# Attention in a decoder layer: projections cut into pieces, one rope step moved back, and the output weights' low parts taken from VectorE to GpSimd

## The chip, the cores and the metric

One core of a Trainium2 chip runs the whole kernel. The metric is device time in microseconds (us) of one execution; three runs of the kernel before gave 1610.72, 1613.61 and 1617.08, median 1613.61. A difference of 0.5% is about 8 us.

## What is computed

The reference is one pre-norm decoder layer on x of shape (4, 512, 512) in float32: causal grouped-query attention, a cross attention to 64 memory tokens, and a mixture of 8 experts. The change touches the first part alone:

```python
def _L0_attn_ref(x, Wq, Wk, Wv, Wo):                  # 32 query heads, 8 key/value heads, 64 wide
    q = (x @ Wq.T).reshape(B, L, HQ, HD)
    k = (x @ Wk.T).reshape(B, L, HKV, HD)
    v = (x @ Wv.T).reshape(B, L, HKV, HD)
    q = _rope(q)
    k = _rope(k)
    ...
    attn = jnp.einsum('bkgqd,bkld->bkgql', qh, kh) * SCALE
    attn = jnp.where(causal[None, None, None], attn, -jnp.inf)
    p = jax.nn.softmax(attn, axis=-1)
    out = jnp.einsum('bkgql,bkld->bkgqd', p, vh)
    ...
    return out @ Wo.T

x = x + _L0_attn_ref(_layernorm(x, axis=-1), L0_attn_Wq, L0_attn_Wk, L0_attn_Wv, L0_attn_Wo)
```

## The kernel before

The attention is written out by hand, engine by engine, with semaphores between them. Its outer loop is over the 8 key/value heads ("groups", g), then over the 4 batches (b), then over the 4 query heads (h) of that group: 8 x 16 = 128 **steps** c, each on one head of 64 columns and 512 rows. Every engine's program walks the same steps in `pe_group`, `act_group`, `dve_group` and `pool_group`; in step c the score matmuls are those of head c + 1, the transposes of P those of head c - 1 (in the code `d = c - 1`, with its batch `db` and its head `dh`), and P times v that of head c - 2. What stands in one engine's program is done in that order, and no engine overtakes.

Float32 accuracy is had by splitting a value into a high part (rounded by a copy on ScalarE, ACT) and a low part (value minus high part, one subtraction on VectorE, DVE, or GpSimd, POOL), and multiplying in two or three passes on TensorE (PE). The work of one step:

- PE: transposes of unit 2 of P (2 blocks, `pe_ptrans` L218), scores (`pe_scores`, 8 matmuls, L208), a projection (`pe_proj`, 12 matmuls, L185) where one falls in the step, transposes of units 0 and 1 (8 blocks, L218), P times v (`pe_pv`, 8 matmuls, L235), and one of the four 128-row tiles of a batch's output projection (`pe_wo`, 6 matmuls, L247).
- DVE: four masked row blocks (`dve_masked` L422), the low parts of P transposed (`dve_pt`, `pt_lo`, L410), the reciprocal of row sums (L429), sums for the output (`dve_oadd` L475, `dve_woacc` L485), low parts of q (L447, L448), of o and v, and the first half of rope (`dve_rope_in` L440, L441: times cosine, and a shuffle into `rot`).
- ACT: the high parts (`act_split` L306) and the exponentials (`act_exp` L313).
- POOL: the second half of rope (`pool_rope` L537, L539: `rot` times sine, then the sum), the softmax scaling of P (`pool_norm` L546), the low part of k (`pool_k_lo` L553).

A group has three projections for each batch, each made one batch ahead: r = 2 (k and v together) in step h = 0, r = 0 and r = 1 (two query heads each) in steps h = 1 and h = 2. Each of the three has a rope step behind it, numbered by h; the third is the one of step h = 2. Step h = 3 has no projection; there v is transposed (`pe_vt` L195). All projections go through one PSUM bank, `PJ_BANK`, so a projection waits until rope has read the one before. Rope's second halves wait on one `rot` buffer.

Weights of a group come in by DMA while the group before runs: `w1` (for q, k, v) and `w2` (the group's 256 rows of the output weights, 512 columns). There is one buffer for `w2`: `act_w2` can write its high parts only after the last output tile of the group before (step h = 1 of b = 1, c = 5), and PE needs high and low parts for the first output tile of the group, in step h = 2 of b = 1 (c = 6). In the kernel before the low parts are `dve_w2`, in that step on DVE:

```python
                if h == 2 and next_batch:
                    dve_q_lo(dve, m + 1, 1, (b + 1) % 2)
                if dh == 1 and db == 1:
                    dve_w2(dve, g)
                if h < 3 and next_batch:
                    dve_rope_in(dve, m + 1, h, (b + 1) % 2)
```

PE waits for them in front of that tile, with `pe.wait_ge(s["w2_lo_done"], 2 * g + 2)`. Groups 1 to 6 are a loop of two turns (`Fori`), three groups in each turn.

Of the kernel before, what the change touches and what calls it, by code (L numbers as in the profile page):

```python
# [15 lines left out]
F32 = mybir.dt.float32  # L16
# [9 lines left out]
P = 128  # L26
# [38 lines left out]
W1_SLOTS = {(2, 1): 2, (2, 2): 0, (2, 3): 1}  # L65

# [33 lines left out]
def decoder_layer(nc, x, ctx, ctx_cols, mem_mask, wqkv, wo_rows, router_cols, router_b, gu_w, gu_b, down_w, down_b,  # L100
                  cos_t, sin_t, causal_t, ident_t, iota_t, out):
    stack = ExitStack()
    with stack:
# [76 lines left out]
        def pe_proj(pe, b, r):  # L180

            first = True
            for c in range(DC):
                for sp, mp in PASSES:
                    last = nc.tensor.matmul(PJ_BANK[:, :], w1[sp][:, c, r * P:(r + 1) * P], xn[mp][:, c, b * L:(b + 1) * L],  # L185
                                            start=first, stop=(c == DC - 1 and (sp, mp) == PASSES[-1]))
                    first = False
            last.then_inc(s["proj_done"], 1)

        def pe_vt(pe, m):  # L190

            pe.wait_ge(s["vt_done"], m + 1)
            settled(pe)
            for j in range(QB):
                last = nc.tensor.transpose(PJ_BANK[:, j * HD:(j + 1) * HD], v_t[:, j * P:(j + 1) * P], ident[HD:P, HD:P])  # L195
            last.then_inc(s["v_tr"], 1)
# [55 lines left out]
        def pe_group(pe, g, r):  # L252
# [4 lines left out]
            for c in range(HEADS + (isinstance(g, int) and g == GROUPS - 1)):  # L257
# [12 lines left out]
                d_before_last = not (isinstance(g, int) and g == 0 and db < 2)  # L270
                if d_begun:
# [3 lines left out]
                if h < 3 and b == 3 and next_batch:  # L275
                    pe.wait_ge(s["w1_lo_done"], 3 * g + 4 + h)
                if h == 0 and next_batch:
                    pe.wait_ge(s["v_lo_done"], m + 1)
                    pe_proj(pe, (b + 1) % B, 2)
                if h == 1 and next_batch:  # L280
                    pe.wait_ge(s["rope_in"], 3 * m + 4)
                    pe.wait_ge(s["vt_done"], m + 2)
                    pe_proj(pe, (b + 1) % B, 0)
                if h == 2 and next_batch:
                    pe.wait_ge(s["rope_in"], 3 * m + 5)
                    pe_proj(pe, (b + 1) % B, 1)
                if h == 3 and next_batch:
# [9 lines left out]
                if dh in (1, 2) and d_last:  # L297
                    if dh == 1 and db == 1:
                        pe.wait_ge(s["w2_lo_done"], 2 * g + 2)
                    pe_wo(pe, dm - 1, (db - 1) % 2, dh - 1)  # L300
                if dh == 0 and d_before_last:
                    pe_wo(pe, dm - 2, db % 2, 3)
# [65 lines left out]
        def act_group(act, g, r):  # L368

            for c in range(HEADS + (isinstance(g, int) and g == GROUPS - 1)):  # L370
# [41 lines left out]
        def dve_masked(dve, n, hb):  # L412
# [3 lines left out]
            for i in (3, 2, 1, 0):  # L416
# [1279 lines left out]
```

## Time and profile before

| | |
|---|---|
| median of three runs | 1613.61 us |
| the profiled execution, its own time | 1613.59 us |
| its span in the trace | 1611.8 us |
| busy share of PE, DVE, ACT, POOL in the span | 92%, 85%, 66%, 54% |
| mean granted TensorE clock | 0.958 of 2.4 GHz |

Times in the trace count from the start of the span. The attention takes the span up to about 1045 us, the rest is the cross attention and the experts. A group of 16 steps takes 123 us. Timeline rows give the start, the time that one instruction took (for several merged ones the stretch from the first start to the last end), engine, line, output and inputs, shape, count, and in brackets how long the engine had been idle and who released it. Matmuls are pipelined, so the length of a run of them is read from its first start to the next run's first start.

### The profile page before, as it was taken

The page shows a single profiled execution, that of the slowest core. Times are in us where ns is not written, and L with a number is a line of the kernel's source. Part 1 is how long each engine was busy: PE and PEld are TensorE (multiplying, and loading weights), DVE is VectorE, ACT ScalarE, POOL GpSimd, SP SyncE. Part 2 cuts the span into 40 slices and gives each one's busy share as a digit, 9 for nine tenths or more (in the row PEclk, how much of TensorE's full clock was granted, in tenths as well). Part 3 has the DMA queues.
Part 4 walks back from the last instruction along what each step waited for, and adds up shares of the span by engine and source line. Part 5 has one row for each costly group of instructions (what it writes and reads, how often), then busy time and mean ns, then how long its engine had stood idle before and what let it go on. Part 6 is the DMA issues. An engine that isn't in the chain of part 4 may idle for free. (4 is left out here: it accounts for less than half of the span.)

```text
span 1611.8 us, 31199 instructions
## 1 busy us (share of the span) xinstructions
PE 1484.4 (92%) x8952; PEld 1308.7 (81%) x8952; DVE 1374.7 (85%) x3583; ACT 1056.9 (66%) x2464; POOL 870.1 (54%) x1024
## 2 busy tenths in 40 slices
PE   5789999999999899999999999769879999999998
PEld 4678888888888778887887887658769999999997
DVE  7788898898988798898898888668868888988896
ACT  3677777777777677777777777533136666666664
POOL 6657657557657556656656666157413343334432
PEclk9899999999999999999999999975579999999999
DMA  4000000000000000000000000042448888777761
GB/s 178 1 14 21 1 14 21 1 14 21 1 14 21 3 14 16 6 14 2 21 4 12 1 1 1 1 139 99 133 124 226 227 230 227 228 210 211 202 184 46
DMA packets 61950, 117.10 MB, mean 73 GB/s; under 512 B 22718, under 2 KB 22846, under 8 KB 61776
## 3 DMA queue, kind: packets, MB, share of 16 engines
q1 hardware_dynamic: 51328, 98.05, 19.1%
q0 software_dynamic: 10304, 16.94, 5.2%
q8 instruction: 77, 1.26, 0.3%
q14 instruction: 97, 0.79, 0.1%
q10 hardware_dynamic: 144, 0.07, 0.0%
HBM read 101.89 MB, written 20.51 MB: 76 GB/s over the span
## 5 line engine op out<-in xcount | busy, mean ns | idle before, releaser
L313 ACT ACTIVATE probs<-probs,neg_max 128x512 f32<-128x512 f32 (+3 forms) x512 | 281.6, 551 | 46.5 <-DVE neg_max L422 44.2
L546 POOL TENSOR_SCALAR probs<-probs,row_inv 128x512 f32<-128x512 f32 (+3 forms) x512 | 264.2, 534 | 44.5 <-DVE row_inv L429 44.5
L537 POOL TENSOR_TENSOR rot<-rot,sin 128x512 f32<-128x512 f32 (+1 forms) x96 | 123.7, 1289 | 303.8 <-DVE rot L441 299.4
L218 PE MATMUL bank<-ident,probs 128*128 128x128 f32 x1280 | 185.1, 275 | 59.9 <-DVE pt_lo L410 50.4
L410 DVE TENSOR_TENSOR pt_lo<-bank,pt_hi 128x512 fp32r<-128x512 f32 (+1 forms) x384 | 216.2, 590 | 26.9 <-ACT pt_hi L306 26.9
L1265 POOL DMA_INDIRECT out<-ctx_raw,idx x46 | 93.1, 2024 | 268.6 <-ACT ctx_raw L1420 217.3
L306 ACT ACTIVATE pt_hi<-bank 128x512 fp32r<-128x512 f32 (+1 forms) x384 | 186.0, 518 | 72.8 <-PE bank L218 64.5
L422 DVE CUSTOM_DVE_ANT_0 probs<-bank,causal 128x512 f32<-128x512 f32 (+3 forms) x512 | 219.8, 482 | 10.3 <-issue 3.3
L218 PEld LDWEIGHTS bank<-ident,probs 128*128 128x128 f32 x1280 | 150.5, 141 | 95.2 <-DVE pt_lo L410 55.3
L1347 PE MATMUL bank<-xt_hi,gu_hi 128*128 128x256 f32 x736 | 208.8, 284 | 3.5 <-issue 1.9
L1347 PE MATMUL bank<-xt_hi,gu_lo 128*128 128x256 f32 x736 | 206.9, 281 | 0.0
L1347 PE MATMUL bank<-xt_lo,gu_hi 128*128 128x256 f32 x736 | 206.9, 281 | 0.0
L208 PE MATMUL bank<-k_hi,q_st 128*128 128x256 f32 (+2 forms) x512 | 172.7, 348 | 2.9 <-DVE xn_lo L410 2.9
L235 PE MATMUL bank<-pt_hi,v_st 128*128 128x256 f32 (+2 forms) x512 | 171.1, 345 | 1.6 <-DVE pt_lo L410 1.6
L208 PE MATMUL bank<-k_lo,q_st 128*128 128x256 f32 (+2 forms) x512 | 157.2, 328 | 0.0
L235 PE MATMUL bank<-pt_lo,v_st 128*128 128x256 f32 (+2 forms) x512 | 155.4, 326 | 0.0
L185 PE MATMUL bank<-xn_hi,w_hi 128*128 128x512 f32 x384 | 152.6, 397 | 0.3 <-ACT v_and_o L306 0.3
L185 PE MATMUL bank<-xn_lo,w_hi 128*128 128x512 f32 x384 | 151.4, 394 | 0.0
L185 PE MATMUL bank<-xn_hi,w_lo 128*128 128x512 f32 x384 | 151.0, 393 | 0.0
L1347 PEld LDWEIGHTS bank<-xt_hi,gu_hi 128*128 128x128 f32 x736 | 139.8, 190 | 7.4 <-issue 4.2
L1347 PEld LDWEIGHTS bank<-xt_lo,gu_hi 128*128 128x128 f32 x736 | 140.0, 190 | 3.0
L1347 PEld LDWEIGHTS bank<-xt_hi,gu_lo 128*128 128x128 f32 x736 | 139.7, 190 | 0.0
(204 smaller groups left out, 3920.7 us busy)
## 6 DMA issues: line engine op xcount, KB each, us to landing
gu_raw<-in_gate_up SPq DMA_DIRECT2D x92, 512.0 KB, 3.8
dn_raw<-in_down SPq DMA_DIRECT2D x92, 256.0 KB, 3.8
w_raw<-in_wqkv SPq DMA_DIRECT2D x8, 768.0 KB, 4.1
w_raw<-in_wo_rows SPq DMA_DIRECT2D x8, 512.0 KB, 3.5
h_rows<-ln_h SPq DMA_DIRECT2D x16, 256.0 KB, 2.0
out<-x_res SPq DMA_DIRECT2D x4, 1024.0 KB, 5.0
x_res<-in_x SPq DMA_DIRECT2D x3, 1024.0 KB, 11.1
ctx_raw<-in_ctx SPq DMA_DIRECT2D x2, 512.0 KB, 6.3
```

The lines of the kernel that those rows point to most:

```text
L185: last = nc.tensor.matmul(PJ_BANK[:, :], w1[sp][:, c, r * P:(r + 1) * P], xn[mp][:, c, b * L:(b + 1) * L], start=first, stop=(c == DC - 1 ...
L208: last = nc.tensor.matmul(S_BANK[k][:, at:at + cols], q_st[:, h, i * P:(i + 1) * P], kk[:, kb, 0:cols], start=(a == 0), stop=(a == 1))
L218: last = nc.tensor.transpose(T_BANK[u % 2][:, k * P:(k + 1) * P], probs[:, hb, P_AT[i] + j * P:P_AT[i] + (j + 1) * P], ident[:, :])
L235: last = nc.tensor.matmul(dst, v_st[:, vb, j, :], rhs, start=(j == 0 and a == 0), stop=(j == QB - 1 and a == 1))
L306: nc.scalar.activation(dst, src, ACT.Copy).then_inc(sem_, 1)
L313: nc.scalar.activation(row, row, ACT.Exp, bias=neg_max[:, hb, i:i + 1], scale=-1.0, accum_out=row_sum[:, hb, i:i + 1]).then_inc(s["exp_don ...
L410: nc.vector.tensor_tensor(dst, src, hi.bitcast(F32), ALU.subtract).then_inc(sem_, 1)
L422: nc.vector.tensor_tensor_reduce(out=probs[:, hb, P_AT[i]:P_AT[i] + (i + 1) * P], in0=S_BANK[k][:, at:at + (i + 1) * P], in1=causal[:, (QB ...
L537: nc.gpsimd.tensor_tensor(rot[0:rows, :], rot[0:rows, :], sin[0:rows, :], ALU.mult).then_inc(s["rot_sin"], 1)
L546: nc.gpsimd.tensor_scalar(row, row, row_inv[:, hb, i:i + 1], 0.0, ALU.mult, ALU.add).then_inc(s["pnorm_done"], 1)
L1265: nc.gpsimd.indirect_dma_start(out=out_rows, out_offset=bass.IndirectOffsetOnAxis(ap=idx[:, 2 * tau + h:2 * tau + h + 1], axis=0), in_=y[: ...
L1347: last = nc.tensor.matmul(GU_BANK[u % 3][:, side * TILE:(side + 1) * TILE], gu[sp_][:, ib, c, side, :], xts[mp][:, k, c, :], start=first, ...
```

## The change

1. **Projections in pieces.** `pe_proj` takes a range of its 12 matmuls. The k and v projection is begun in step h = 3 of the batch before (9 matmuls) and ended in h = 0 (3); r = 0 is begun at the end of h = 0 (6) and ended in h = 1 (6); r = 1 is begun at the end of h = 1 (3) and ended in h = 2 (9). Each of the steps then has 9 projection matmuls.
2. **Output tiles.** Tiles 1 and 3 move ahead of the transposes of their steps, as tile 2 was; tile 0 alone (step h = 2) stays behind P times v.
3. **v.** Its transposes go through a bank of the P transposes, `T_BANK[1]`, and move ahead of the scores of step h = 3; its high and low parts move with them, and the next transposes into that bank wait for them.
4. **Rope.** In step h = 2 alone DVE's half (the third rope step) moves behind the low parts of P. The copy of its result on ACT and the low part of q on DVE move from the next h = 0 into h = 3.
5. **DVE order.** The low part of P's unit 2 moves between the second and the third masked block. `act_o` moves to the start of the next step.
6. **w2.** Its low parts move from DVE to POOL (`pool_w2`), behind `pool_norm` of step c = 6. POOL's low parts of w1 get a wait for the low part of q in two of three slots.
7. **No loop.** Groups 1 to 6 are written out.

```diff
+KV_FIRST, Q01_FIRST, Q23_FIRST = 9, 6, 3
...
-        def pe_vt(pe, m):
+        def pe_vt(pe, m, heads_before):
             pe.wait_ge(s["vt_done"], m + 1)
             settled(pe)
+            wait(pe, s["pt_lo_done"], heads_before and 3 * heads_before - 1)
...
+            if u == 1 and n % G == 2 and n < HEADS * GROUPS - G:
+                pe.wait_ge(s["v_lo_done"], n // G + 2)
...
+                if h == 3 and next_batch:
+                    pe_vt(pe, m + 1, dn_)
                 if more:
                     pe_scores(pe, n + 1, m if h < G - 1 else m + 1, (h + 1) % G, (b + (h == G - 1)) % 2)
...
                 if h == 0 and next_batch:
-                    pe.wait_ge(s["v_lo_done"], m + 1)
-                    pe_proj(pe, (b + 1) % B, 2)
+                    pe_proj(pe, (b + 1) % B, 2, KV_FIRST)
                 if h == 1 and next_batch:
...
-                    pe_proj(pe, (b + 1) % B, 0)
+                    pe_proj(pe, (b + 1) % B, 0, Q01_FIRST)
                 if h == 2 and next_batch:
...
+                    pe_proj(pe, (b + 1) % B, 1, Q23_FIRST)
+                if h == 3 and batch_after:
+                    if b == 2:
+                        pe.wait_ge(s["w1_lo_done"], 3 * g + 4)
                     pe.wait_ge(s["rope_in"], 3 * m + 6)
-                    pe_vt(pe, m + 1)
+                    pe_proj(pe, (b + 2) % B, 2, 0, KV_FIRST)
                 if dh == 3 and d_last:
                     pe_wo(pe, dm - 1, (db - 1) % 2, 2)
+                if dh == 2 and d_last:
+                    pe_wo(pe, dm - 1, (db - 1) % 2, 1)
+                if dh == 0 and d_before_last:
+                    pe_wo(pe, dm - 2, db % 2, 3)
                 if d_here:
                     pe_ptrans(pe, dn_, (r + d) % 3, 0)
                     pe_ptrans(pe, dn_, (r + d) % 3, 1)
...
+                if dh == 1 and d_last:
+                    if db == 1:
                         pe.wait_ge(s["w2_lo_done"], 2 * g + 2)
+                    pe_wo(pe, dm - 1, (db - 1) % 2, 0)
+                if h == 0 and next_batch:
+                    if b == 3:
+                        pe.wait_ge(s["w1_lo_done"], 3 * g + 5)
+                    pe.wait_ge(s["rope_in"], 3 * m + 4)
+                    pe.wait_ge(s["vt_done"], m + 2)
+                    pe_proj(pe, (b + 1) % B, 0, 0, Q01_FIRST)
+                if h == 1 and next_batch:
...
+                    pe.wait_ge(s["rope_in"], 3 * m + 5)
+                    pe_proj(pe, (b + 1) % B, 1, 0, Q23_FIRST)
...
-                if h == 0 and begun and front:
-                    act_rope(act, m, 2, b % 2)
-                if h in (1, 2) and next_batch:
+                e = d - 1
+                eb, eh = divmod(e, G)
+                if eh % 2 == 0 and not (isinstance(g, int) and g == 0 and e < 1):
+                    act_o(act, HEADS * g + e - 1, B * g + eb if eh else B * g + eb - 1, (e // 2 - 1) % 4)
+                if h == 3 and next_batch:
+                    act_v(act, m + 1, (b + 1) % 2)
+                if h and next_batch:
                     act_rope(act, m + 1, h - 1, (b + 1) % 2)
...
+        def pool_w2(pool, g):
             for k in range(2):
-                dve.wait_ge(s["w2_hi_done"], 2 * g + k + 1)
-                dve_lo(w2[1][:, k, :], w2_raw[:, k, :], w2[0][:, k, :], s["w2_lo_done"])
+                pool.wait_ge(s["w2_hi_done"], 2 * g + k + 1)
+                nc.gpsimd.tensor_tensor(w2[1][:, k, :], w2_raw[:, k, :], w2[0][:, k, :].bitcast(F32), ALU.subtract).then_inc(s["w2_lo_done"], 1)
...
                 if more:
-                    dve_masked(dve, n + 1, (r + c + 1) % 3)
+                    dve_masked(dve, n + 1, (r + c + 1) % 3, (3, 2))
                 if d_begun:
                     dve_pt(dve, dn_ - 1, (d + 1) % 2, 2)
+                if more:
+                    dve_masked(dve, n + 1, (r + c + 1) % 3, (1, 0))
...
-                if dh == 1 and db == 1:
-                    dve_w2(dve, g)
-                if h < 3 and next_batch:
+                if h == 3 and next_batch:
+                    dve_v(dve, m + 1, (b + 1) % 2)
+                if h >= 2 and next_batch:
+                    dve_q_lo(dve, m + 1, h - 1, (b + 1) % 2)
+                if h < 3 and next_batch and h != 2:
                     dve_rope_in(dve, m + 1, h, (b + 1) % 2)
...
                     dve_pt(dve, dn_, d % 2, 0)
                     dve_pt(dve, dn_, d % 2, 1)
+                if h == 2 and next_batch:
+                    dve_rope_in(dve, m + 1, h, (b + 1) % 2)
...
                 if more:
                     pool_norm(pool, n + 1, (r + c + 1) % 3)
+                if dh == 1 and db == 1:
+                    pool_w2(pool, g)
                 if (b, h) in W1_SLOTS and not (isinstance(g, int) and g == GROUPS - 1):
+                    if h < 3:
+                        pool.wait_ge(s["q_lo_done"], 2 * m + 2 + h)
                     w1_lo(nc.gpsimd, pool, g + 1, W1_SLOTS[b, h])
...
-                with pe.Fori(0, (GROUPS - 2) // 3) as q:
-                    for i in range(1, 4):
-                        pe_group(pe, 3 * q + i, i % 3)
+                for g in range(1, GROUPS - 1):
+                    pe_group(pe, g, g % 3)
```

What the diff does to the order, at three places. The square brackets name the semaphores that an instruction waits for.

POOL, step c = 6 of a group (shown for group 0), before: the second half of the third rope step (`rot`, `rope`), then the softmax scaling of one head (`probs`).

```order
L537 TENSOR_TENSOR rot<-rot,sin 128x512 [waits rope_in]
L539 TENSOR_TENSOR rope<-rope,rot 128x512 [waits rot_sin]
L546 TENSOR_SCALAR probs<-probs,row_inv 128x512 [waits recip_done]
L546 TENSOR_SCALAR probs<-probs,row_inv 128x384
L546 TENSOR_SCALAR probs<-probs,row_inv 128x256
L546 TENSOR_SCALAR probs<-probs,row_inv 128x128
```

The same step after:

```order
L556 TENSOR_TENSOR rot<-rot,sin 128x512 [waits rope_in]
L558 TENSOR_TENSOR rope<-rope,rot 128x512 [waits rot_sin]
L565 TENSOR_SCALAR probs<-probs,row_inv 128x512 [waits recip_done]
L565 TENSOR_SCALAR probs<-probs,row_inv 128x384
L565 TENSOR_SCALAR probs<-probs,row_inv 128x256
L565 TENSOR_SCALAR probs<-probs,row_inv 128x128
L480 TENSOR_TENSOR w_lo<-w_raw,w_hi 128x512 [waits w2_hi_done] x2
```

The two low parts of w2 are new on POOL and stand last in the step, behind the rope sum and the scaling.

DVE, step h = 2 of b = 0 in group 0, from the low part of P's unit 2 on, before (at c = 6 the two `w_lo` of w2 stand between `q_st` and `rope`):

```order
L410 TENSOR_TENSOR pt_lo<-bank,pt_hi 128x256 [waits pt_hi_done]
L410 TENSOR_TENSOR o_lo<-o_f,o_hi 128x512 [waits o_hi_done]
L447 TENSOR_TENSOR q_st<-rope,q_st 64x512 [waits rope_hi]
L448 TENSOR_TENSOR q_st<-rope,q_st 64x512
L440 TENSOR_TENSOR rope<-bank,cos 128x512 [waits k_lo_done,rope_sum,proj_done]
L441 STREAM_SHUFFLE rot<-bank 128x512
L429 RECIPROCAL row_inv<-row_sum 128x4 [waits exp_done]
L410 TENSOR_TENSOR pt_lo<-bank,pt_hi 128x512 [waits pt_hi_done] x2
```

and the end of that step after:

```order
L427 TENSOR_TENSOR o_lo<-o_f,o_hi 128x512 [waits o_hi_done]
L464 TENSOR_TENSOR q_st<-rope,q_st 64x512 [waits rope_hi]
L465 TENSOR_TENSOR q_st<-rope,q_st 64x512
L446 RECIPROCAL row_inv<-row_sum 128x4 [waits exp_done]
L427 TENSOR_TENSOR pt_lo<-bank,pt_hi 128x512 [waits pt_hi_done] x2
L457 TENSOR_TENSOR rope<-bank,cos 128x512 [waits k_lo_done,rope_sum,proj_done]
L458 STREAM_SHUFFLE rot<-bank 128x512
```

The shuffle into `rot`, for which POOL's first row above waits, went from ahead of the reciprocal to behind the two low parts of P.

ACT, step h = 3, after (before, the two `q_st` copies stood in the next step, h = 0, and `v_st` behind `pt_hi` of units 0 and 1):

```order
L323 ACTIVATE pt_hi<-bank 128x256 [waits ptrans_done]
L323 ACTIVATE v_st<-bank 128x4x64 [waits pv_done,v_tr]
L323 ACTIVATE q_st<-rope 64x512 [waits scores_done,rope_sum]
L323 ACTIVATE q_st<-rope 64x512
L330 ACTIVATE probs,row_sum<-probs,neg_max 128x512 [waits masked_done]
L330 ACTIVATE probs,row_sum<-probs,neg_max 128x384 [waits masked_done]
L330 ACTIVATE probs,row_sum<-probs,neg_max 128x256 [waits masked_done]
L330 ACTIVATE probs,row_sum<-probs,neg_max 128x128 [waits masked_done]
L323 ACTIVATE pt_hi<-bank 128x512 [waits pv_done,ptrans_done]
```

The copies of the third rope result (`q_st`, released by POOL's `rope_sum`) now stand ahead of the step's exponentials and of `pt_hi`.

## Rows read from the trace of the kernel before

**Rows 1.** Busy time by engine in a stretch of the attention: PE, PEld, DVE, ACT, POOL, clock.

```profile
160.00:540.00 380.00, 361.11 (x2077) 312.49 (x2075) 339.10 (x894) 289.17 (x733) 241.14 (x307) 1.00 0.04 12
```

**Rows 2.** Waits of PE from 60 to 1046 us: total us, times, longest.

```profile
PE bank L218 <- DVE pt_lo L410: 50.4, 48, 3.7
```

**Rows 3.** Timeline of PE: v's transposes of three batches, and a step h = 2.

```profile
288.71 0.46 PE L195 MATMUL bank<-ident,v_and_o 64*128 64x64 f32 x4
...
309.52 0.38 PE L218 MATMUL bank<-ident,probs 128*128 128x128 f32 x2
...
311.03 0.40 PE L185 MATMUL bank<-xn_hi,w_hi 128*128 128x512 f32 x1
...
313.77 1.03 PE L218 MATMUL bank<-ident,probs 128*128 128x128 f32 x8
...
315.94 0.40 PE L247 MATMUL bank<-w_hi,o_hi 128*128 128x512 f32 x1
...
317.32 0.38 PE L218 MATMUL bank<-ident,probs 128*128 128x128 f32 x2
...
318.93 0.46 PE L195 MATMUL bank<-ident,v_and_o 64*128 64x64 f32 x4
...
320.55 1.09 PE L218 MATMUL bank<-ident,probs 128*128 128x128 f32 x8 [1.16 <-DVE pt_lo L410]
...
534.84 0.46 PE L195 MATMUL bank<-ident,v_and_o 64*128 64x64 f32 x4
```

**Rows 4.** Timeline of PE around the loop's turn, after group 3.

```profile
552.19 0.49 PE L218 MATMUL bank<-ident,probs 128*128 128x128 f32 x2 [2.61 <-DVE pt_lo L410]
...
554.88 0.63 PE L185 MATMUL bank<-xn_hi,w_hi 128*128 128x512 f32 x1
...
558.11 1.03 PE L218 MATMUL bank<-ident,probs 128*128 128x128 f32 x8
...
571.04 0.46 PE L195 MATMUL bank<-ident,v_and_o 64*128 64x64 f32 x4
```

**Rows 5.** Waits of all engines, 60 to 1060 us: the one on ACT without a releaser.

```profile
ACT pt_hi L306 <- issue: 5.5, 1, 5.5
```

**Rows 6.** Busy time by engine behind that turn; the column after POOL is the granted clock.

```profile
552.50:555.50 3.00, 3.00 (x12) 2.71 (x11) 2.77 (x8) 2.40 (x7) 2.92 (x6) 0.50 0.00 0
```

**Rows 7.** Timeline of PE and ACT at c = 6 of a group, begun at 339.74.

```profile
339.74 0.38 PE L218 MATMUL bank<-ident,probs 128*128 128x128 f32 x2
...
340.43 1.14 ACT L306 ACTIVATE w_hi<-w_raw 128x512 fp32r<-128x512 f32 x2
...
341.88 1.27 ACT L306 ACTIVATE q_st<-rope 64x512 fp32r<-64x512 f32 x2
343.18 0.73 ACT L313 ACTIVATE probs<-probs,neg_max 128x512 f32<-128x512 f32 x1
...
345.38 1.05 ACT L306 ACTIVATE pt_hi<-bank 128x512 fp32r<-128x512 f32 x2
```

**Rows 8.** Timeline of DVE in the same step.

```profile
340.73 0.69 DVE L422 CUSTOM_DVE_ANT_0 probs<-bank,causal 128x512 f32<-128x512 f32 x1
...
342.71 0.80 DVE L410 TENSOR_TENSOR o_lo<-o_f,o_hi 128x512 fp32r<-128x512 f32 x1
...
344.97 1.29 DVE L410 TENSOR_TENSOR w_lo<-w_raw,w_hi 128x512 fp32r<-128x512 f32 x2
346.18 0.68 DVE L440 TENSOR_TENSOR rope<-bank,cos 128x512 f32<-128x512 f32 x1
...
347.50 1.26 DVE L410 TENSOR_TENSOR pt_lo<-bank,pt_hi 128x512 fp32r<-128x512 f32 x2
```

**Rows 9.** Timeline of POOL in the same step.

```profile
347.61 1.28 POOL L537 TENSOR_TENSOR rot<-rot,sin 128x512 f32<-128x512 f32 x1 [4.62 <-DVE rot L441]
...
350.24 2.06 POOL L546 TENSOR_SCALAR probs<-probs,row_inv 128x512 f32<-128x512 f32 x4
```

**Rows 10.** Low parts of weights by tile, 180 to 540 us: ns min/median/max.

```profile
L457 POOL TENSOR_TENSOR w_lo<-w_raw,w_hi x9: 1283/1297/1724, 251.3 to 511.3; 128x512 fp32r<-128x512 f32 x9
```

More of the change, by code:

```diff
@@ L178, in pe_ln, with pe_proj @@
             last.then_inc(s["lnt_done"], 1)
[L180 to L188, printed above, removed]
-        def pe_vt(pe, m):
+        def pe_proj(pe, b, r, begin=0, end=3 * DC):
+            for n in range(begin, end):
+                c, (sp, mp) = n // 3, PASSES[n % 3]
+                last = nc.tensor.matmul(PJ_BANK[:, :], w1[sp][:, c, r * P:(r + 1) * P], xn[mp][:, c, b * L:(b + 1) * L],
+                                        start=(n == 0), stop=(n == 3 * DC - 1))
+            if end == 3 * DC:
+                last.then_inc(s["proj_done"], 1)
+        def pe_vt(pe, m, heads_before):
             pe.wait_ge(s["vt_done"], m + 1)
             settled(pe)
+            wait(pe, s["pt_lo_done"], heads_before and 3 * heads_before - 1)
             for j in range(QB):
-                last = nc.tensor.transpose(PJ_BANK[:, j * HD:(j + 1) * HD], v_t[:, j * P:(j + 1) * P], ident[HD:P, HD:P])
+                last = nc.tensor.transpose(T_BANK[1][:, j * HD:(j + 1) * HD], v_t[:, j * P:(j + 1) * P], ident[HD:P, HD:P])
             last.then_inc(s["v_tr"], 1)
@@ L410, in dve_lo, with dve_masked @@
             nc.vector.tensor_tensor(dst, src, hi.bitcast(F32), ALU.subtract).then_inc(sem_, 1)
-        def dve_masked(dve, n, hb):
+        def dve_masked(dve, n, hb, blocks=(3, 2, 1, 0)):
             wait(dve, s["ptrans_done"], 3 * n - 6)
-            for i in (3, 2, 1, 0):
+            for i in blocks:
                 k = (2, 2, 1, 0)[i]
@@ L521, in dve_group @@
                     dve_pt(dve, dn_, d % 2, 1)
+                if h == 2 and next_batch:
+                    dve_rope_in(dve, m + 1, h, (b + 1) % 2)
                 if dh == 3 and d_last:
                     dve_woacc(dve, dm - 1, (db - 1) % B, 2)
-                if h == 3 and next_batch:
-                    dve_v(dve, m + 1, (b + 1) % 2)
+                if dh == 2 and d_last:
+                    dve_woacc(dve, dm - 1, (db - 1) % B, 1)
+                if dh == 0 and d_before_last:
+                    dve_woacc(dve, dm - 2, (db - 2) % B, 3)
                 if d_begun:
                     dve_oadd(dve, dn_ - 1, (d - 1) % 2, HEADS // 2 * g + (d - 1) // 2)
-                if dh in (1, 2) and d_last:
-                    dve_woacc(dve, dm - 1, (db - 1) % B, dh - 1)
-                if dh == 0 and d_before_last:
-                    dve_woacc(dve, dm - 2, (db - 2) % B, 3)
+                if dh == 1 and d_last:
+                    dve_woacc(dve, dm - 1, (db - 1) % B, 0)
         def pool_rope(pool, m, r, mb):
@@ L607, in _ @@
                 sp_w2(sp, 0)
-                with sp.Fori(1, GROUPS) as g:
+                for g in range(1, GROUPS):
                     sp_w1(sp, g)
@@ L667, in _ @@
                 act_group(act, 0, 0)
-                with act.Fori(0, (GROUPS - 2) // 3) as q:
-                    for i in range(1, 4):
-                        act_group(act, 3 * q + i, i % 3)
+                for g in range(1, GROUPS - 1):
+                    act_group(act, g, g % 3)
                 act_group(act, GROUPS - 1, (GROUPS - 1) % 3)
@@ L709, in _ @@
                 dve_group(dve, 0, 0)
-                with dve.Fori(0, (GROUPS - 2) // 3) as q:
-                    for i in range(1, 4):
-                        dve_group(dve, 3 * q + i, i % 3)
+                for g in range(1, GROUPS - 1):
+                    dve_group(dve, g, g % 3)
                 dve_group(dve, GROUPS - 1, (GROUPS - 1) % 3)
@@ L738, in _ @@
                 pool_group(pool, 0, 0)
-                with pool.Fori(0, (GROUPS - 2) // 3) as q:
-                    for i in range(1, 4):
-                        pool_group(pool, 3 * q + i, i % 3)
+                for g in range(1, GROUPS - 1):
+                    pool_group(pool, g, g % 3)
                 pool_group(pool, GROUPS - 1, (GROUPS - 1) % 3)
```

31 lines of the change are left out of this document (7 added, 24 removed).

## Prediction

> **What bounds the kernel now.** I read the busy shares by stretch first. In the steady attention PE is busy 361 of 380 us (95%), DVE 339 (89%), ACT 289, POOL 241 [rows 1]: PE is the bound, DVE close behind, POOL has room. The granted clock is full there. Next the waits of PE: 48 waits for a low part of P, 50.4 us in all, are nearly everything [rows 2]. So the question is what PE's own work takes and what stands between.
>
> The timeline of PE answers it. A step h = 2 runs without a hole from 309.52 to 317.32, 7.80 us: unit 2 and scores 1.51, twelve projection matmuls 2.74, the transposes of units 0 and 1 with P times v 2.17, an output tile 1.38 [rows 3]. Step h = 3 has no projection but v's transposes (0.46): 7.80 - 2.74 + 0.46 = 5.52. A batch without any wait is then 3 x 7.80 + 5.52 = 28.92 us, a group 115.68. What it takes is read from v's transposes: 288.71 to 318.93 is 30.22 for a batch without weight work, of which 1.16 is the one wait in front of the transposes in h = 3, where PE has too little to do while DVE still masks; 288.71 to 534.84 is two groups, 123.07 each [rows 3]. **The loss is 7.39 us a group**, 59 in eight. That is all that a better order can give back.
>
> One thing comes on top: the loop's turn. The batch from 534.84 to 571.04 takes 36.20 instead of 30.22 [rows 3, 4], 5.98 more. ACT stands 5.5 us without any releaser there [rows 5], PE 2.61 [rows 4], and behind it the clock is at 0.50, 1.2 GHz [rows 6], so that unit 2 and scores take 2.69 instead of 1.51 and the projection 3.23 instead of 2.74 [rows 3, 4]: 1.7 us is the price of a slow clock after a gap.
>
> **The change, part by part.** I write times from the start of a step on PE.
>
> *Pieces, output tiles, v.* No matmul is added or taken away. Four steps of 9 projection matmuls (2.05 us) replace three of 12; every step is about 7.12, h = 3 with v's transposes 7.58. The batch's sum stays 28.92. What can change is the waits.
>
> *Loop written out:* -6.0 us, once. The two groups from 288.71 to 534.84 [rows 3] run through code written out inside a turn, at one pace, so I cost the longer code at nothing.
>
> *The third rope step.* It now starts on DVE behind the low parts of P. In a plain batch's h = 2 POOL's queue ahead (rope, scaling, low part of k, rope: 2.63 + 2.06 + 2.6 + 2.63 [rows 9, 10] from the first rope's shuffle, some 5.8 into h = 0) lets ACT copy q at about 1.8; the copies take 1.30 and the exponentials 2.20 [rows 7], so pt_hi begins at 5.3, its low parts are done at 7.1 (0.6 for one pt_hi, 1.2 for two low parts [rows 8]) and rope's half on DVE, 1.24 [rows 8], at 8.3. POOL's half ends at 8.4 + 2.63 = 11.1. In h = 3 ACT must now copy that result before its exponentials: copies to 12.5, exponentials to 14.7, one pt_hi 15.2, its low part 15.9, and for that PE waits at the next h = 0, which it would reach at 7.12 + 7.58 = 14.7. **A wait of about 1.3 us returns, at another place**, where 1.16 stood before. Bounds: nothing if ACT's part comes 1.3 earlier, 2.6 if it comes as much later. I take 1.3: every term of it is a row.
>
> *w2 on POOL.* DVE loses 2 x 0.6 us at c = 6 (344.97 to 346.18 [rows 8]); POOL gets two subtractions at 1.30 [rows 10]. POOL has the room on average. But look at what stands ahead of them in its queue, and what waits. POOL reaches w2 in step c = 6 behind the third rope's half and the scaling; that rope waits for DVE's shuffle, which now comes behind the low parts of P; and PE needs w2's low parts in the same step, behind P times v:
> - ACT: the w2 copies begin at 0.1 (o_hi, ahead of them before, moves behind them). Before, from them to pt_hi of unit 0 it took 340.43 to 345.38, 4.95 [rows 7]; with o_hi in it (0.53, half of the two pt_hi copies of that shape [rows 7]) pt_hi begins at 5.6.
> - DVE: masks from 1.0 (340.73 - 339.74 [rows 7, 8]), to o_lo 1.98, o_lo and the low part of q 2.26, free at 5.2; low parts of P from 6.2 (one pt_hi is 0.53) to 7.4; rope 1.24, to 8.6 [rows 8].
> - POOL: rope 2.63 (347.61 to 350.24), to 11.3 with 0.09 in front; scaling 2.06, to 13.4 [rows 9]; w2 2.6 [rows 10], to 16.0.
> - PE is ready at 1.51 + 2.05 + 2.17 = 5.7 and **stands 10.3 us**, once a group.
>
> Bounds: if ACT held nobody up, pt_lo would follow q's low part at 5.2 and all ends 1.0 earlier, 9.3; if ACT came a set of exponentials later (2.2), 12.5. In either case DVE's order alone puts the shuffle behind PE's transposes. In that gap ACT, DVE and POOL work off what they owe, so the 1.3 us of this batch vanishes. After it PE starts at the slow clock: I take the 1.7 us of the loop's turn; the ends are 0 and 3.4.
>
> *w1.* After, its copies stand at ends of steps where ACT next waits for rope anyway, and POOL's new wait for q's low part (5.2 of h = 2) ends before its next rope can begin (8.4): nothing. If that cover were gone, 1.3 us, one subtraction [rows 10], once a group.
>
> *Sum.* A group loses 10.3 + 1.7 + 3 x 1.3 = 15.9 us instead of 7.4, 8.5 more; eight are 68; the loop gives back 6. 1613.6 + 62 = **1676 us**. The profiled execution took 1613.59 us, 1.8 more than its span, and the median is 1613.61, so nothing has to be converted. The rest of the kernel is left alone.
>
> **What the Trainium skill says.** The GPSIMD Engine Reference, sections 3.1 and 4.1, gives VectorE for elementwise work on a tile, GpSimd being 1.96 times slower in a two-input add: a rule against this move. By it the pair would take 1.96 x 1.29 = 2.5 us (an estimate from that page) where the rows of POOL give 2.6, and the sum would be 1 us less; trace and page agree that the move doubles this work, but its length is a quarter of the gap and its place in the queue the rest. On the clock, TensorE: Matmul & The Clock Gate, Part 1, says that "the default state is throttled, and activity releases the throttle"; the row at 0.50 behind a 2.61 us gap agrees. By that rule each of the eight gaps must pay, as I have it; without it the sum would be 14 us less.
>
> **Rivals.**
> 1. *The late rope costs nothing in plain batches.* For it: steps are balanced, DVE's mask order brings P's unit 2 forward. Against: ACT's exponentials in h = 3 now wait for POOL. 24 waits of 1.3 less: 1676 - 31 = 1645.
> 2. *The waits are larger than I count.* DVE is at 89%, and a late step pushes the next. Plain waits of 2.6 instead of 1.3: 1676 + 31 = 1707.
> 3. *Faster: w2 is in time.* If POOL had w2 done by 5.7 us of c = 6, all the loss could go: 1613.6 - 59 - 6 = 1549. For it: POOL was idle 4.62 us in just that step [rows 9]. Against: it was idle in front of the rope, waiting for the shuffle, and w2 stands behind that. The point that decides: with no other wait left, gap and slow clock together would have to be under 7.4 + 0.75 = 8.1 us; my lowest gap alone is 9.3.
> 4. *PE does not wait there after all*, because w2's low parts come from the group before. The code writes them anew for each group and PE's wait counts them, so I give this little; it falls together with the third.
>
> **How the numbers follow.** Forecast 0.74, first rival 0.12, second 0.10, third and fourth 0.04. The range 1640 to 1710 takes in the first two rivals and, for the forecast, gaps of 9.3 to 12.5 (-8 to +18) and clock prices of 0 to 3.4 (-14 to +14), not all at one end. Slower by over 0.5% (8 us, what a measurement of this kernel can tell from no change) 0.95; within 0.5% 0.02, a gap near the deciding point; faster 0.03.
>
> **What would show it.** PE's waits: eight of about 10 us in front of the first output tile, for `w_lo`, released by POOL's L480; POOL's `w_lo` starting some 13.4 us after the step does; 1.2 GHz behind each; the waits for `pt_lo` moved from the transposes of units 0 and 1 to unit 2 of h = 0, about 1.3 us, 24 of them; no 5.5 us hole on ACT. It is wrong if `w_lo` on POOL starts before the rope's half, if the gaps are under 8 us, or if a batch without weights takes 29 us or over 32.

## The result, and the profile after

The changed kernel takes 1688.74 us (median of 4 runs, 1686.61 to 1690.56), the kernel before beside it 1615.34 (4 runs). The ratio is 1.0444 with an interval of 1.0415 to 1.0473: **4.4% slower, 73 us**, where +62 had been forecast. The profiled execution took 1687.77 us, 1.9 more than its span of 1685.9; the span grew by 74.1.

The page after: the line of the span, the busy shares, and of the costliest groups the output projection on PE (after the second bar: idle time in front of the group, and what ended most of it).

```profile
span 1685.9 us, 28647 instructions
...
PE 1505.6 (89%) x8952; PEld 1321.4 (78%) x8952; DVE 1368.5 (81%) x3567; ACT 1066.6 (63%) x2464; POOL 914.0 (54%) x1040
...
L252 PE MATMUL bank<-w_hi,o_hi 128*128 128x512 f32 x256 | 105.8, 413 | 83.3 <-POOL w_lo L480 80.2
```

POOL's share is 54%, as it was before. An average did not see the loss; the last line does. PE stood 80.2 us in front of output tiles, and the end of POOL's low parts of w2 released it.

Waits of all engines after, 60 to 1125 us (total us, times, longest):

```profile
PE bank L252 <- POOL w_lo L480: 80.2, 8, 10.7
ACT q_st L323 <- POOL rope L558: 67.2, 25, 3.1
...
PE bank L223 <- DVE pt_lo L427: 30.2, 26, 2.7
```

Eight waits of 10.0 us are new, one a group. The 48 waits for a low part of P, 50.4 us [rows 2], are now 26, 30.2 us; 21 of them, three between each two of the eight, are 1.0 to 1.1 us long, and the other five lie at the two ends of the attention. ACT's 5.5 us without a releaser [rows 5] is gone from this list. The second line is nearly new on ACT: its copies of q wait for POOL's rope, which before they did once, for 1.6 us.

Now step c = 6 of group 2, which starts on PE at 360.66; it answers to [rows 7, 8, 9]. PE, from v's transposes of the batch before on:

```profile
337.66 0.46 PE L198 MATMUL bank<-ident,v_and_o 64*128 64x64 f32 x4
...
360.66 0.38 PE L223 MATMUL bank<-ident,probs 128*128 128x128 f32 x2
...
366.28 0.28 PE L240 MATMUL bank<-pt_lo,v_st 128*128 128x256 f32 x1
376.48 0.79 PE L252 MATMUL bank<-w_hi,o_hi 128*128 128x512 f32 x1 [9.92 <-POOL w_lo L480]
...
379.21 0.63 PE L223 MATMUL bank<-ident,probs 128*128 128x128 f32 x2
379.77 0.69 PE L198 MATMUL bank<-ident,v_and_o 64*128 64x64 f32 x4
...
382.21 0.40 PE L187 MATMUL bank<-xn_hi,w_hi 128*128 128x512 f32 x1
...
409.58 0.46 PE L198 MATMUL bank<-ident,v_and_o 64*128 64x64 f32 x4
...
470.59 0.46 PE L198 MATMUL bank<-ident,v_and_o 64*128 64x64 f32 x4
```

DVE and then POOL in the same step:

```profile
366.73 1.29 DVE L427 TENSOR_TENSOR pt_lo<-bank,pt_hi 128x512 fp32r<-128x512 f32 x2 [0.30 <-ACT pt_hi L323]
367.94 0.68 DVE L457 TENSOR_TENSOR rope<-bank,cos 128x512 f32<-128x512 f32 x1
...
368.54 0.72 DVE L458 STREAM_SHUFFLE rot<-bank 128x512 f32<-128x512 f32 x1
```

```profile
369.34 1.26 POOL L556 TENSOR_TENSOR rot<-rot,sin 128x512 f32<-128x512 f32 x1 [4.53 <-DVE rot L458]
370.69 1.26 POOL L558 TENSOR_TENSOR rope<-rope,rot 128x512 f32<-128x512 f32 x1
371.92 2.06 POOL L565 TENSOR_SCALAR probs<-probs,row_inv 128x512 f32<-128x512 f32 x4
373.94 2.48 POOL L480 TENSOR_TENSOR w_lo<-w_raw,w_hi 128x512 fp32r<-128x512 f32 x2
```

Read them as one chain. POOL stands idle 4.53 us until the shuffle ends, then does rope, scaling and w2 in its queue's order; PE, done at 366.56 (366.28 + 0.28), starts its tile when w2 ends. The change moved the chain's start, the shuffle, back, and put at the chain's end the low parts for which PE waits; before, PE's list has one wait for them in the whole kernel, of 1.1 us, ended by DVE.

Busy time by engine in four stretches of this step (PE, PEld, which is PE's weight load, DVE, ACT, POOL, granted clock, DMA share, GB/s):

```profile
366.40:371.00 4.60, 0.16 (x2) 0.00 (x0) 3.12 (x7) 1.37 (x3) 1.58 (x2) 1.00 0.00 0
371.20:376.40 5.20, 0.00 (x0) 0.00 (x0) 0.00 (x0) 0.00 (x0) 5.20 (x7) 0.50 0.00 0
376.50:381.30 4.80, 4.80 (x14) 3.57 (x15) 0.69 (x1) 1.19 (x3) 0.00 (x0) 0.50 0.36 113
381.40:386.00 4.60, 4.60 (x26) 3.95 (x25) 3.95 (x13) 2.92 (x9) 0.12 (x1) 1.00 0.00 0
```

For 5.2 us POOL alone of the five works. The clock is at 0.50 (1.2 GHz) for that time and for 4.8 us more, in which PE is busy throughout.

### The profile page after: what moved, and what is told of

It is laid out like the page before. It is cut to its first block and busy times, and to the rows that moved or that the text cites. A ratio compares the mean times of both kernels' runs of the same rounds, so it can differ in the third digit from the quotient of the medians.

```text
span 1685.9 us, 28647 instructions
## 1 busy us (share of the span) xinstructions
PE 1505.6 (89%) x8952; PEld 1321.4 (78%) x8952; DVE 1368.5 (81%) x3567; ACT 1066.6 (63%) x2464; POOL 914.0 (54%) x1040
## 5 line engine op out<-in xcount | busy, mean ns | idle before, releaser
L565 POOL TENSOR_SCALAR probs<-probs,row_inv 128x512 f32<-128x512 f32 (+3 forms) x512 | 288.9, 585 | 119.3 <-DVE row_inv L446 119.3
L439 DVE CUSTOM_DVE_ANT_0 probs<-bank,causal 128x512 f32<-128x512 f32 (+3 forms) x512 | 228.3, 482 | 20.5 <-PE bank L211 18.6
L223 PE MATMUL bank<-ident,probs 128*128 128x128 f32 x1280 | 185.2, 275 | 30.5 <-DVE pt_lo L427 30.2
L252 PE MATMUL bank<-w_hi,o_hi 128*128 128x512 f32 x256 | 105.8, 413 | 83.3 <-POOL w_lo L480 80.2
L187 PE MATMUL bank<-xn_hi,w_hi 128*128 128x512 f32 x384 | 156.3, 407 | 3.0 <-ACT v_and_o L323 2.4
L502 DVE TENSOR_TENSOR x_res<-bank,x_res 128x512 f32<-128x512 f32 x128 | 87.0, 680 | 80.2 <-PE bank L252 80.2
```

Of the source, the lines that this page charges most:

```text
L223: last = nc.tensor.transpose(T_BANK[u % 2][:, k * P:(k + 1) * P], probs[:, hb, P_AT[i] + j * P:P_AT[i] + (j + 1) * P], ident[:, :])
L439: nc.vector.tensor_tensor_reduce(out=probs[:, hb, P_AT[i]:P_AT[i] + (i + 1) * P], in0=S_BANK[k][:, at:at + (i + 1) * P], in1=causal[:, (QB ...
L565: nc.gpsimd.tensor_scalar(row, row, row_inv[:, hb, i:i + 1], 0.0, ALU.mult, ALU.add).then_inc(s["pnorm_done"], 1)
```

## The experiments

The ratios are to the kernel before, run beside each; its medians there were 1614.5 to 1616.6 us, so times of different experiments can be compared to about 2 us. An edit "to the change" starts from the changed kernel.

### Is it w2's place? Four runs

**e3_before_w2_pool**: the kernel before, with nothing but w2's low parts moved.

```diff
...
-                if dh == 1 and db == 1:
-                    dve_w2(dve, g)
...
                     pool_norm(pool, n + 1, (r + c + 1) % 3)
+                if dh == 1 and db == 1:
+                    pool_w2(pool, g)
```

> The kernel before with w2's low parts on POOL, behind the scaling, and nothing else changed: rope is early, the loop stays. Theory: at c = 6 the shuffle ends at 6.5, rope at 9.2, scaling at 11.3, w2 at 13.9, PE is ready at 6.4: a gap of 7.5 us and 2.4 us of slow clock in place of the 2.5 us lost there before, 7.4 more eight times: about 1674 us. Rival (the late rope makes all of the gap): about 1615 us or a little less, since DVE has less to do.

Measured: 1682.56 us (1677.46 to 1684.81), ratio 1.0402 [1.0374, 1.0431]. PE's waits:

```profile
PE bank L247 <- POOL w_lo L463: 59.2, 8, 8.3
```

This one move costs 4.0% by itself. Its gap is 7.4 us, 59.2 / 8; in the change, where the rope is late too, it is 10.0. The time is 9 us above the expected 1674: the 2.5 us that the step lost before were taken as gone, but in the step traced here a wait of 1.06 us behind the gap stays.

**e1_w2_on_dve**: to the change, w2's low parts back on DVE.

```diff
...
+                if dh == 1 and db == 1:
+                    dve_w2(dve, g)
                 if h < 3 and next_batch and h != 2:
                     dve_rope_in(dve, m + 1, h, (b + 1) % 2)
...
-                if dh == 1 and db == 1:
-                    pool_w2(pool, g)
```

> The changed kernel with w2's low parts back on DVE, in the place they had before; all else changed. Theory (PE stands because w2's low parts wait in POOL's queue behind the late rope): the eight gaps of 10.0 us and the 2.4 us of slow clock behind each go, the step gets back a wait of about 1.2 us in front of the next head and about 1.2 us for the two subtractions on DVE, so 1689 - 8 x 12.4 + 8 x 2.4 = about 1609 us. Rival (the pieces, the moved output tiles and the late rope cost the time themselves): stays above 1660 us.

Measured: 1604.69 us (1603.24 to 1606.80), ratio 0.9928 [0.9910, 0.9947]: 84 us under the change, and 0.7% faster than before. PE's wait for w2 is 0.9 a group:

```profile
PE bank L252 <- DVE w_lo L427: 7.1, 8, 1.3
```

**e2_w2_first**: to the change, w2 stays on POOL, but ahead of rope in the same step.

```diff
+                if dh == 1 and db == 1:
+                    pool_w2(pool, g)
                 if h < 3 and next_batch:
                     pool_rope(pool, m + 1, h, (b + 1) % 2)
                 if more:
                     pool_norm(pool, n + 1, (r + c + 1) % 3)
-                if dh == 1 and db == 1:
-                    pool_w2(pool, g)
```

> The changed kernel with w2's low parts still on POOL, but ahead of the rope's half in that step. Theory (place in the queue): POOL starts them when the scaling of the step before ends, some 3.7 us into the step, and ends at about 6.3, PE is ready at 5.7: a gap of 0.6 us and no slow clock, so 1689 - 8 x 12.4 + 8 x 1.8 = about 1604 us. Rival (the work is simply too slow on POOL, twice DVE's time, wherever it stands): half of the gap or more remains, 1640 us or above.

Measured: 1604.75 us (1600.71 to 1609.99), ratio 0.9925 [0.9899, 0.9950]. PE's wait, and w2 on POOL in this kernel:

```profile
PE bank L252 <- POOL w_lo L480: 14.3, 8, 2.6
```

```profile
345.68 3.39 POOL L480 TENSOR_TENSOR w_lo<-w_raw,w_hi 128x512 fp32r<-128x512 f32 x2
```

The same two subtractions on the same engine cost 1.8 us a group in this place and 10.0 in the other. So it is not POOL's speed that makes the gap, but the place in its queue. Half of the remaining 1.8 has a reason of its own, told with the last points below.

**e7_w2_middle**: to the change, w2 between rope and scaling. This only takes the scaling's 2.06 us out of the chain.

```diff
                     pool_rope(pool, m + 1, h, (b + 1) % 2)
-                if more:
-                    pool_norm(pool, n + 1, (r + c + 1) % 3)
                 if dh == 1 and db == 1:
                     pool_w2(pool, g)
+                if more:
+                    pool_norm(pool, n + 1, (r + c + 1) % 3)
```

> The changed kernel with w2's low parts on POOL between the rope's half and the softmax scaling. Theory (the gap is the length of the queue ahead): it shrinks by the scaling, 2.06 us, to 8.0 us, eight times: 1689 - 16 = 1673 us, with the slow clock's price as it is. Rival (the subtractions themselves or another wait): unchanged, 1689 us.

Measured: 1666.27 us (1664.15 to 1669.01), ratio 1.0306 [1.0284, 1.0328]. PE's waits, and its timeline behind one gap:

```profile
PE bank L252 <- POOL w_lo L480: 63.7, 8, 8.6
```

```profile
369.89 0.79 PE L252 MATMUL bank<-w_hi,o_hi 128*128 128x512 f32 x1 [7.88 <-POOL w_lo L480]
...
372.61 0.63 PE L223 MATMUL bank<-ident,probs 128*128 128x128 f32 x2
373.17 0.46 PE L198 MATMUL bank<-ident,v_and_o 64*128 64x64 f32 x4
```

The gap is 8.0, shorter by 2.06: a step of the chain removed is removed from the gap. The time fell by 22 us and not by 16. For the other 6 the rows show a reason: v's transposes are back at 0.46 here (0.69 in the change), so the clock has risen again by 373.17. From 369.89 to there it is 3.28 us for tile and unit 2, which take 1.70 at full clock, so this gap's price is 1.6 where the change paid more (e8, next).

### What does the slow clock cost?

**e8_fill_gap**: to the change, 40 matmuls whose result the tile overwrites, in front of the wait for w2, so that PE stays busy while the end of the wait depends on POOL as before.

```diff
                     if db == 1:
+                        wait(pe, s["wo_out_done"], 4 * (dm - 1))
+                        for i in range(40):
+                            nc.tensor.matmul(WO_BANK[:, :], w1[0][:, i % DC, 0:P], xn[0][:, i % DC, 0:L], start=True, stop=True)
                         pe.wait_ge(s["w2_lo_done"], 2 * g + 2)
```

> The changed kernel with 40 matmuls of 512 columns on PE in front of the wait for w2's low parts, their result overwritten by the output tile that follows (work added, none left out). They take 40 x 0.227 = 9.1 us of the 10.0 us gap. Theory: the gap's end does not move, only the slow clock behind it goes: 1689 - 8 x 2.4 = about 1669 us, the granted clock 1.00 through the step. Rival (the 2.4 us behind the gap are matmuls waiting for other engines): 1689 us or more.

Measured: 1670.36 us (1668.37 to 1676.02), ratio 1.0346 [1.0313, 1.0378], 18.4 us under the change. The filled gap and its clock (columns as in the stretches above):

```profile
363.01 9.25 PE L309 MATMUL bank<-xn_hi,w_hi 128*128 128x512 f32 x40
373.19 0.50 PE L252 MATMUL bank<-w_hi,o_hi 128*128 128x512 f32 x1 [0.93 <-POOL w_lo L483]
```

```profile
368.50:375.50 7.00, 6.07 (x30) 4.55 (x29) 0.61 (x1) 0.39 (x2) 4.63 (x7) 1.00 0.18 49
```

PE does useless work and the kernel gets 1% faster: 18.4 / 8 = **2.3 us a gap is the price of the slow clock**. The trace of the change gives the same: from the tile's start to the next projection, 376.48 to 382.21, it is 5.73 us, against 1.38 + 0.32 + 0.39 + 1.38 = 3.47 for tile, unit 2, v's transposes and scores in steps of the change at full clock, 2.3 more. By the two profiled executions alone (1687.77 and 1672.15) it would be 2.0.

### What does the late rope cost?

**e4_rope_early**: to the change, DVE's half of the third rope step back to its old place; w2 stays last on POOL.

```diff
-                if h < 3 and next_batch and h != 2:
+                if h < 3 and next_batch:
                     dve_rope_in(dve, m + 1, h, (b + 1) % 2)
...
-                if h == 2 and next_batch:
-                    dve_rope_in(dve, m + 1, h, (b + 1) % 2)
```

> The changed kernel with the third rope step back in its early place on DVE (ahead of the reciprocal); w2 stays last on POOL. Theory: the shuffle ends at 6.5 instead of 8.6 of the step, so the gap shrinks by about 2 us to 8.0; and the copies of q on ACT no longer hold up the exponentials of h = 3, so the 24 waits of 1.1 us at the next h = 0 go, and some 0.45 us at v's transposes comes: 1689 - 16 - 24 x 0.7 - a little slow clock = about 1653 us. Rival (those waits come from DVE being full, not from the order on ACT): the gap shrinks alone, about 1670 us.

Measured: 1652.31 us (1650.10 to 1653.26), ratio 1.0225 [1.0198, 1.0253], 36 us under the change. PE's waits:

```profile
PE bank L252 <- POOL w_lo L480: 65.1, 8, 8.5
PE bank L223 <- DVE pt_lo L427: 9.4, 25, 1.8
```

The gap lost 1.9 us, and the waits for `pt_lo` fell from 30.2 to 9.4. A plain batch takes 29.7 here (v's transposes at 269.99, 299.74, 329.45) and 30.5 in the change (409.58 to 440.08). The change's ACT and PE in h = 3 and the step behind it show how the late rope makes that wait:

```profile
413.30 1.29 ACT L323 ACTIVATE q_st<-rope 64x512 fp32r<-64x512 f32 x2 [2.84 <-POOL rope L558]
414.62 0.72 ACT L330 ACTIVATE probs<-probs,neg_max 128x512 f32<-128x512 f32 x1
...
416.82 1.05 ACT L323 ACTIVATE pt_hi<-bank 128x512 fp32r<-128x512 f32 x2
```

```profile
415.58 0.48 PE L240 MATMUL bank<-pt_hi,v_st 128*128 128x512 f32 x1
...
418.17 0.44 PE L223 MATMUL bank<-ident,probs 128*128 128x128 f32 x2 [1.06 <-DVE pt_lo L427]
418.37 0.48 PE L211 MATMUL bank<-k_hi,q_st 128*128 128x512 f32 x1
```

ACT stands 2.84 us for POOL's sum with the exponentials queued behind it, and PE meets the delay at 418.17. From P times v to unit 2 it takes PE 2.59 us (415.58 to 418.17) where it takes 1.37 without a wait, and from unit 2 to the scores 0.20 instead of 0.14: the wait of 1.06 in the list costs 1.3 us from start to start.

**e5_both**: e2 and e4 together.

> The changed kernel with both moves: w2 first on POOL in its step, and the third rope step early. Theory: 1604.8 (w2 first alone) less 28 waits of 1.1 that become 0.45: about 1586 us. Rival (the waits at h = 0 come from DVE being full): no gain over 1604.8, or a loss since the low parts of P come 0.6 us later.

Measured: 1586.58 us (1583.56 to 1588.78), ratio 0.9820 [0.9795, 0.9845]. The waits are 14.4 for w2 and 8.3 for `pt_lo`. The two costs nearly add: 84 and 36 us alone, 102 together. Most of the 18 that lack are the 15 us (80.2 to 65.1) that the early rope took from w2's gap in e4, and that are not there to be taken where w2 stands first.

### The best version, and a miss

**e10_w2_dve_rope_early**: e1 and e4 together.

> The same pieces and the early rope, with w2's low parts on DVE as before the change. If DVE's time is the scarce one in that step, the 1.2 us there push the low parts of P and PE loses about as much as POOL's remaining gap of 1.8 us: about 1586 us. If DVE has room, about 1573 us.

Measured: 1580.77 us (1579.22 to 1587.88), ratio **0.9790 [0.9767, 0.9813]**, the best of all: 2.1% under before and 6.4% under the change. PE's waits are 8.2 us for `pt_lo` and 7.2 for w2. That lies between the two expected times, so it does not decide whether DVE has room. The rest of the change (pieces, output tiles, v, DVE's order, no loop) is worth 34 us, and the two moves, w2 onto POOL and the third rope step behind the low parts of P, take away 108.

**e9_w2_step_sooner**: with the early rope, w2 on POOL one step sooner, in c = 5, so that PE should not wait for it at all.

```diff
                     pool_rope(pool, m + 1, h, (b + 1) % 2)
+                if dh == 0 and db == 1:
+                    pool_w2(pool, g)
                 if more:
                     pool_norm(pool, n + 1, (r + c + 1) % 3)
-                if dh == 1 and db == 1:
-                    pool_w2(pool, g)
```

> The version with the third rope step early, and w2's low parts on POOL a step sooner (c = 5), between that step's rope and its scaling. Theory (queue): w2's high parts are ready at about 8.4 of that step, POOL's rope there ends at 8.8, so the low parts end at 11.4, which is 4.3 of step c = 6 where PE needs them at 5.7: no gap at all, and the rope of c = 6 is not held up. 1586.6 - 8 x 1.8 = about 1572 us. Rival (POOL has no room for it): the wait moves to the scaling or the rope behind it and the time stays at 1587 us or more.

Measured: 1590.30 us (1588.82 to 1594.94), ratio 0.9837 [0.9815, 0.9859]: a miss. The wait for w2 is gone, as expected, but a wait for `pt_lo` stands one step later. All waits for `pt_lo`, then PE, DVE and POOL there:

```profile
PE bank L223 <- DVE pt_lo L427: 22.6, 34, 2.0
```

```profile
347.34 0.44 PE L223 MATMUL bank<-ident,probs 128*128 128x128 f32 x2 [1.58 <-DVE pt_lo L427]
```

```profile
341.49 1.70 DVE L427 TENSOR_TENSOR o_lo<-o_f,o_hi 128x512 fp32r<-128x512 f32 x1
343.22 1.07 DVE L464 TENSOR_TENSOR q_st<-rope,q_st 64x512 fp32r<-64x512 f32 x1
344.30 0.98 DVE L465 TENSOR_TENSOR q_st<-rope,q_st 64x512 fp32r<-64x512 f32 x1
```

```profile
342.62 3.37 POOL L563 TENSOR_SCALAR probs<-probs,row_inv 128x512 f32<-128x512 f32 x4
```

In e5 the waits were 8.3 us for `pt_lo` and 14.4 for w2: the second sum came back as waits of the first kind. w2 pushed the scaling of P back until it ran beside DVE's three low parts (the first of them ran beside the end of w2, too). These take 3.75 us here and 0.90 + 0.75 + 0.69 = 2.34 in the same step of e10, where the scaling ends 0.2 us into the second; the scaling takes 3.37 where it took 2.06 alone. DVE has no idle time from there to its low parts of P, so PE gets them late. That is read from the rows; no run undid this overlap alone.

### The loop

**e6_before_no_loop**: the kernel before, with groups 1 to 6 written out in every engine's program, the loop of SyncE's weight loads too, and nothing else.

```diff
...
-                with pe.Fori(0, (GROUPS - 2) // 3) as q:
-                    for i in range(1, 4):
-                        pe_group(pe, 3 * q + i, i % 3)
+                for g in range(1, GROUPS - 1):
+                    pe_group(pe, g, g % 3)
```

> The kernel before with groups 1 to 6 written out instead of the loop, and nothing else. Theory: the loop's turn cost 6.0 us once and code written out costs nothing: 1616.6 - 6 = about 1611 us, no hole of 5.5 us on ACT. Rival (longer code has to be fetched): 1617 us or more, with holes without releaser elsewhere.

Measured: 1613.40 us (12 runs, 1609.40 to 1632.49), ratio 1.000 [0.9976, 1.0024]: a miss. In its profiled execution, of 1625.38 us, the batch of 36.2 us and ACT's hole are gone, but two batches in each of five groups take 32.8 and 32.3 instead of 31.2 and 30.6.

**e11_before_no_loop_again**: the same kernel, for the trace of a second execution.

> The kernel before with the loop written out, once more, for a trace of an execution that is not the one of 1625 us. If the loop's turn was worth its 6 us and the 1625 us execution had slow clocks of its own, this one shows batches of 30.2 to 31.2 us, no batch of 36, and 1609 to 1613 us.

Measured: 1623.39 us (1 run): a miss as well. PE's waits, one of them in the timeline, and the stretches ahead of it and behind it:

```profile
PE bank L218 <- POOL probs L546: 44.3, 30, 1.7
PE bank L218 <- DVE pt_lo L410: 15.6, 22, 3.8
```

```profile
357.72 1.94 PE L218 MATMUL bank<-ident,probs 128*128 128x128 f32 x8 [1.73 <-POOL probs L546]
```

```profile
354.00:357.50 3.50, 1.99 (x14) 1.63 (x14) 3.50 (x12) 1.65 (x5) 3.42 (x5) 1.00 0.21 87
357.70:361.00 3.30, 3.28 (x13) 3.11 (x14) 1.54 (x4) 2.30 (x7) 2.29 (x5) 0.50 0.00 0
```

Both profiled executions show it: waits of 1.7 us for POOL's scaling, with the clock at 0.50 behind. With the loop, waits for the scaling sum to 8.8 us and waits for `pt_lo` to 50.4 [rows 2], 59.2 together, and here to 59.9: the waits were exchanged, not lengthened. What the rows show as new is the slow clock behind them. Ten batches of e6 are 1.6 or 1.7 us longer, some 16 in all; less the 6 of the loop's turn that is near the 12 by which its profiled execution is slower. Why the written-out program falls into these waits, and whether the faster unprofiled runs do, stays open.

## Why the prediction was right, and where two sizes were off

**The mechanism and the place held.** In the step, counted from PE's start of c = 6: low parts of P done at 7.4 (forecast 7.4), shuffle 8.6 (8.6), rope's sum 11.3 (11.3), scaling 13.3 (13.4), w2 and PE's resumption 15.8 (16.0). PE was ready at 5.9 (5.7). The gap is 10.0 us against 10.3, eight times. That the place in the queue makes it was shown from three sides: alone it costs 4.0% (e3), undone it gives 84 us (e1), and moved forward on the same engine it gives the same 84 (e2).

**The plain waits held too.** There are 21 where 24 were forecast, at unit 2 of h = 0, three between each two gaps, and each costs 1.3 us from start to start (e4) as forecast. The chain to them came out as written: counted from 402.14, where that step h = 2 starts on PE, POOL's sum ends at 11.1 (forecast 11.1), `pt_hi` begins at 14.7 (14.7), and PE goes on at 16.0 (15.9). The cause named, ACT's copies behind POOL's rope, falls away with the early rope (e4). Rival 1, that the late rope costs nothing, is refuted by e1 against e10: 24 us. Rival 2 did not come: the waits are no larger. Rival 3 was wrong for this kernel, but its mechanism is real: where w2 is in time or nearly so, the kernel is faster than before (e2, e5, e9, and e10 with w2 on DVE), though not as far down as 1549. Rival 4 falls with the eight waits. That the batch of the gap loses its plain wait was half right: the wait ahead of the gap stays, and the batch behind it takes 29.8 (379.77 to 409.58) instead of 30.5.

**Two terms were mis-sized**, and they make up the 11 us missing. One is "After it PE starts at the slow clock: I take the 1.7 us of the loop's turn". It is 2.3 (e8, and the rows of the change): the gap here is longer, and the clock is still at 0.50 for 4.8 us of work behind it, where the loop's turn was the nearest row at hand [rows 6]. Eight times 0.6 is 5 us.

**The larger one** is "The batch's sum stays 28.92", by which the moved pieces cost nothing. A group, from v's transposes at 337.66 to 470.59, is 132.93 us, 17.25 over the 115.68 of PE's own work; I had 15.9. Of it 10.1 is the gap (PE's matmuls of that shape start 0.12 apart, so the tile would have started at 366.40 and not at 366.56), 3.8 the three plain waits at 1.3, 2.3 the clock. That leaves 1.1 in holes too short for the list of waits, where I had none: 9 us in eight groups. They stand at two places that the change moved. From unit 2 to v's transposes it is 0.32 (409.26 to 409.58), where from unit 2 to the scores it is 0.14 (360.66 to 360.80); the transposes themselves then take 0.39 to the scores instead of the 0.46 I had, so this is some 0.1 a batch. The six matmuls of r = 0 begun at the end of h = 0 take 1.47 to 1.49, the same number in h = 1 1.37 or 1.38: 0.1 a batch, and up to 0.1 more in front of them. Which of the waits of `pe_vt` and of that projection makes the holes was not tried. Against the 14 us of both terms stand 2 from the gap and 1 from the plain waits, which came out a little smaller than forecast.

**The loop's 6 us** fit the sum here: 8 x (132.93 - 123.07) = 79, less 6 is 73, and the span grew by 74. But e6 shows that it is no saving one can count on by itself: taken alone, it came to nothing that could be measured, and a ratio of 0.9963, which 6 us would be, lies outside the interval.

## What to carry to other kernels

Before work is moved to an engine that is idle on average, write down three times for the one step concerned: when its inputs are there, what stands ahead of it in the new queue and when that ends, and when its reader is ready. Here the reader was ready at 5.9 us and the queue at 13.3, and two subtractions of 1.3 us cost 10, and 2.3 more by the slow clock behind; placed ahead of the queue's wait they cost 1.8. And a wait taken away may only uncover the next one (e9): cost what the moved work pushes, too.

## What the runs showed that I had not expected

**DVE and POOL slow each other in some pairs.** In e9 a subtraction of 64x512 on DVE took 1.07 us beside POOL's scaling, 0.69 in e10 with POOL idle. In e2 it is w2 itself: its two subtractions took 3.39 us where they took 2.48 in the gap of the change, and the low part of q beside them was slow as well. DVE in that step of e2:

```profile
345.50 0.74 DVE L464 TENSOR_TENSOR q_st<-rope,q_st 64x512 fp32r<-64x512 f32 x1
346.25 1.69 DVE L465 TENSOR_TENSOR q_st<-rope,q_st 64x512 fp32r<-64x512 f32 x1
```

That is 0.9 us of e2's remaining 1.8. The slow ones read both operands from SBUF (not all of these are as slow: the first line above took 0.74). Those with one operand in a PSUM bank are not slowed in the rows at hand: the two `pt_lo` of the change took 1.29 with POOL idle at 366.73, and 1.26 beside POOL's rope in the kernel before [rows 8, 9]. The Trainium skill, SBUF — State Buffer, section "Who interferes with whom", says that a DVE instruction with two SBUF inputs contends with a GpSimd instruction that reads SBUF, and that one with at most one does not, outside DVE's two-port modes. The rows agree in which instructions are slow; whether the contention is an exclusive lock, as the page says, no run here shows.

**The clock fell behind a short wait, but not behind every one.** In e11 it is at 0.50 behind a wait of 1.73 us. In e2, behind a wait of 1.64 us for w2, it stays at 1.00:

```profile
349.20:352.00 2.80, 2.80 (x15) 2.17 (x16) 2.54 (x6) 0.77 (x2) 1.28 (x1) 1.00 0.62 177
```

What makes the difference these runs do not show. In the change it is 1.00 up to 371.00 and 0.50 from 371.20, inside the gap; in e8, with PE busy on matmuls that nobody reads, it stays at 1.00. The forecast had taken the slow clock for a cost behind the gap alone, and 5 of its 10 us here lie in the gap, where they cost nothing.
